# Attention scores of two batches on eight 32x64 tiles of the array, softmax and value products by pairs

## What is computed

```python
x = x + _L0(x, itok_B_1_198, weights0)          # a picked 32x32 matrix mixes the tokens of each batch
x = x + _L1(x, Wq, Wk, Wv, Wo, ..., k_blocks, v_blocks, block_tables, kv_lens)
x = x + _L2(x, itok_B_0_7, weights2)            # the same as L0 with another table
x = x + _L3(x, W, A, Bm, scalings, adapter)     # x W^T plus a low-rank adapter of rank 16

# _L1, attention over a paged cache: 8 heads in 4 groups of 2, 32 wide
q = _rope(_rms(q, q_norm_scale), pos); k = _rope(_rms(k, k_norm_scale), pos)
k_blocks = k_blocks.at[blk, :, off, :].set(k.transpose(0, 2, 1, 3))   # v_blocks too
scores = jnp.einsum('bghtd,bgsd->bghts', qg, k_all) * SCALE
allowed = (kpos <= pos) & (kpos > pos - 128)
p = jax.nn.softmax(jnp.where(allowed, scores, -jnp.inf), axis=-1)
o = jnp.einsum('bghts,bgsd->bghtd', p, v_all)
return jnp.einsum('bto,do->btd', o, Wo)
```

## Time and profile before

| | us |
|---|---|
| median of 3 runs | 550.79 |
| lowest and highest | 548.58, 552.23 |
| the profiled execution | 547.58 |
| its span (first to last instruction) | 545.8 |
| TensorE busy | 465.9 (85%) |
| VectorE busy | 404.1 (74%) |
| ScalarE busy | 341.7 (63%) |
| GpSimd busy | 209.5 (38%) |

### The profile page before, as it was taken

One profiled execution on the slowest core, in us unless ns is written; L12 is line 12 of the kernel. 1 busy time (PEld: TensorE's weight loads), 2 busy tenths in 40 slices (PEclk: granted clock), 3 DMA queues, 4 the chain that ended last, 5 costly groups with the idle time before them and its releaser, 6 DMA issues.

```text
span 545.8 us, 15661 instructions
## 1 busy us (share of the span) xinstructions
PE 465.9 (85%) x4726; PEld 388.8 (71%) x4726; DVE 404.1 (74%) x1357; ACT 341.7 (63%) x1075; POOL 209.5 (38%) x236
## 2 busy tenths in 40 slices
PE   0667999970026999999999999999999999999996
PEld 0556899960015788888878887887888888888884
DVE  7986478945116788888888888888888888878651
ACT  6166444555004687777877777777677786776662
POOL 7452688879604132422415223152341423212000
PEclk9999899995555899999999999999999999999999
DMA  7999566668266586768677696976968779755100
GB/s 228 293 335 377 174 220 196 193 187 184 82 154 127 139 177 168 170 154 168 165 147 173 144 174 156 152 175 136 170 165 153 170 144 178 173 122 114 22 22 19
DMA packets 87752, 90.10 MB, mean 165 GB/s; under 512 B 24199, under 2 KB 83623, under 8 KB 84940
## 3 DMA queue, kind: packets, MB, share of 16 engines
q1 hardware_dynamic: 72352, 52.58, 40.1%
q0 software_dynamic: 9312, 31.58, 24.4%
q10 hardware_dynamic: 6056, 5.54, 3.1%
HBM read 78.02 MB, written 35.65 MB: 208 GB/s over the span
## 4 chain that ended last, share of the span: by engine, by line
issue 46%; PE 12%; POOL 10%; DMA 3%; POOLq 1%; ACT 1%; DVE 0%; ACTq 0%; DVEq 0%
POOL old L862 4%; PE bank L1329 3%; DMA new<-written_blocks,g_idx 3%; POOL new L871 3%; POOL rms L828 3%; PE bank L1340 2%; PE bank L1355 2%; PE bank L1312 1%; POOL g_idx L855 1%; PE bank L1293 1%; PE bank L1307 1%; PE bank L1313 1%; PE bank L1330 1%; PE bank L1301 1%; PE bank L1288 0%
## 5 line engine op out<-in xcount | busy, mean ns | idle before, releaser
L828 POOL TENSOR_TENSOR rms<-rms,halfpow 128x8 f32<-128x8 f32 x48 | 85.6, 1783 | 232.6 <-DVE rms L576 232.6
L1131 ACT ACTIVATE p_room<-bank,nmax 128x176 f32<-128x176 f32 x256 | 101.4, 404 | 78.8 <-DVE nmax L704 67.1
L1329 PE MATMUL bank<-blocks_room,qbd 128*128 128x176 f32 x512 | 128.3, 355 | 3.4 <-issue 2.6
L1329 PEld LDWEIGHTS bank<-blocks_room,qbd 128*128 128x128 f32 x512 | 79.0, 195 | 22.7 <-issue 3.6
L704 DVE TENSOR_REDUCE nmax<-bank 128x2 f32<-128x352 f32 x128 | 66.7, 521 | 20.9 <-PE bank L1330 18.1
L1340 PE MATMUL bank<-ident,p_room 128*88 128x128 f32 x512 | 78.8, 277 | 3.2 <-DVE p_room L749 2.5
L1144 ACT ACTIVATE pT_room<-bank 88x512 f32<-88x512 f32 x128 | 75.2, 587 | 0.4 <-PE bank L1340 0.4
L749 DVE TENSOR_SCALAR p_room<-p_room,rrec 128x176 f32<-128x176 f32 x256 | 70.4, 317 | 5.6
L1340 PEld LDWEIGHTS bank<-ident,p_room 128*88 128x88 f32 x512 | 58.0, 124 | 14.7 <-DVE p_room L749 7.0
L1330 PE MATMUL bank<-pen,mask_sel 128*128 128x176 bf16 x256 | 62.2, 243 | 0.0
L1288 PE MATMUL bank<-ident,new 88*128 88x88 f32 x256 | 32.1, 252 | 33.3 <-DMA new<-written_blocks,g_idx 33.2
(11 more groups left out here) (199 smaller groups left out, 943.6 us busy)
## 6 DMA issues: line engine op xcount, KB each, us to landing
values_by_group<-new SPq DMA_DIRECT2D x16, 704.0 KB
blocks_room<-values_by_group SPq DMA_DIRECT2D x64, 88.0 KB
v_room<-values_by_group SPq DMA_DIRECT2D x64, 88.0 KB
xin<-in_x_dram SPq DMA_DIRECT2D x32, 128.0 KB
x_spill<-v_room SPq DMA_DIRECT2D x32, 128.0 KB
q_spill<-v_room SPq DMA_DIRECT2D x32, 128.0 KB
written_blocks<-new ACTq DMA_DIRECT2D x2, 2048.0 KB, 8.9
blocks_room<-q_spill SPq DMA_DIRECT2D x32, 128.0 KB
```

Source lines behind the costliest of these rows:

```text
L828: pool.tensor_tensor(out=rms[:, i, 2, :], in0=rms[:, i, 1, :], in1=halfpow[:, :], op=ALU.pow).then_inc(s_rstd, 1)
L1131: last = a.activation(pex[k % 2][:, h, :], ps_s[k % 2][:, h * KEYS:(h + 1) * KEYS], ACT.Exp, bias=nmax[:, k % 4, h:h + 1], accum_out=rsum[ ...
L1329: mm(dst, qbd[grp % 2][:, f, h, :], kT[grp % 2][:, f, :, :, :].rearrange("p c o w -> p (c o w)"), start=True, stop=False)
```

## The change

Slots now come in pairs: even slots compute the scores of two batches, odd slots turn their probabilities over.

- The scores of batches k and k+1 (L1336 and L1340 of the new code) use rows of the array by group and columns by batch: 8 tiles of 32x64 (32 values of a head dimension, 2 heads x 32 tokens), 176 columns each. A bank holds one group; the masks come first, one per bank, with weights of 128 and bf16. `qbd` with its zeros goes, `qT` is written with one copy per tile (L1163) in place of four.
- The four banks of a pair (`ps_u`) take its scores and then its transposed probabilities. So TensorE waits at the masks for both copies of the pair before (`s_ptc`), where it waited for an older exponential.
- Maxima of a pair are two instructions, one per half (two groups). The exponentials stay four per pair, and the transposes eight, of unnormalised probabilities `pex`.
- Normalisation moves behind the value products: VectorE spreads 1/sum over 32 columns (`rrep`), TensorE transposes it (L1377), ScalarE copies it per tile of four batches (`norm`, L1126), and VectorE multiplies the value products with it on their way out, where ScalarE copied them.
- The value products of a pair stand in the even slot behind the next pair's scores, 16 matrices of 88x32.
- The finishing steps come earlier, x2, x3, xa, x4 in slots 1, 2, 3, 0 of four; x3 is copied by VectorE. Keys are prepared in slots 1, 2, 3 and 5 and share one bank; x4, x3 and qT share another, x2 and xa the third. LAST is 133.
- ScalarE reorders values in slots 7 (two pieces) and 1 (two), both odd; VectorE as before.

The core of the diff:

```diff
+        pex = proom[:, 0:G * KEYS].rearrange("p (g k) -> p g k", g=G)
+        pT = troom[0:HK, :].rearrange("p (g c r) -> p g c r", g=G, c=2)
-        qbd = [sb(f"qbd{i}", [128, GB, HPG, 128]) for i in range(2)]
+        qT = [sb(f"qT{i}", [128, GB, HPG, C]) for i in range(2)]
-        ps_s, ps_p, ps_o, ps_m = ps[0:2], [ps[2], ps[4]], ps[5], [ps[6], ps[7], ps[3]]
+        ps_u = [ctx.enter_context(nc.psum_tensor(f"score_banks{i}", [128, 2, 512], f32)) for i in range(2)]
+        ps_o, ps_m = ps[5], [ps[6], ps[7], ps[4]]
-        PREP = {0: [("k0", None)], 1: [("k1", None)], 2: [("k2", None)], 3: [("qT", 0)], 4: [("k3", None)], 7: [("qT", 1)]}
+        PREP = {1: [("k0", None)], 2: [("k1", None)], 3: [("k2", None), ("qT", 0)], 5: [("k3", None)], 7: [("qT", 1)]}
-        FIN = {3: ("x2", 7), 0: ("x3", 8), 1: ("xa", 9), 2: ("x4", 10)}
+        FIN = {1: ("x2", 5), 2: ("x3", 6), 3: ("xa", 7), 0: ("x4", 8)}
+        BANK = {"x4": 0, "x3": 0, "qT": 0, "x2": 1, "xa": 1, "k0": 2, "k1": 2, "k2": 2, "k3": 2}
...
# VectorE
+                if k % 2 == 0 and 0 <= k < B:
+                    dve.wait_ge(s_qk, 8 * it + k // 2 + 1)
+                    for half in range(2):
+                        v.tensor_reduce(nmax[:, k // 2 % 2, 2 * half:2 * half + 2], ps_u[half][:, :, 0:KEYS], AX.X, ALU.max,
+                                        negate=True).then_inc(s_max, 1)
...
+                if k % 4 == 0 and 0 <= (k - 4) // 4 < NT:
+                    n = (k - 4) // 4
+                    dve.wait_ge(s_ntc, 4 * it + n + 1)
+                    dve.wait_ge(s_pv, 8 * it + 2 * n + 2)
+                    v.tensor_tensor(oT[n % 2][:, :, :, :].rearrange("p h f t -> p f h t"),
...
+                if k % 2 == 1 and 0 <= k < B:
+                    j = k // 2
+                    dve.wait_ge(s_exp, b + 1)
+                    v.reciprocal(rrec[:, j % 2, :], rsum[:, j % 2, :]).then_inc(s_rec, 1)
...
+                    v.tensor_copy(rrep[:, j % 2, :].rearrange("p (g d) -> p g d", g=G),
+                                  rrec[:, j % 2, :].unsqueeze(2).broadcast_to([128, G, HD])).then_inc(s_rrep, 1)
...
-                    for h in range(HPG):
-                        last = v.tensor_scalar(pn[k % 2][:, h, :], pex[k % 2][:, h, :], rrec[:, k % 4, h:h + 1], None, ALU.mult)
# ScalarE
+                if k % 4 == 0 and 0 <= (k - 4) // 4 < NT:
+                    n = (k - 4) // 4
+                    act.wait_ge(s_nt, 8 * it + 2 * n + 2)
...
+                    a.activation(norm[n % 2][:, :], ps_o[:, NORM_AT:2 * NORM_AT], ACT.Copy).then_inc(s_ntc, 1)
...
-                i, pieces = pieces_in_slot(k, {6: (0,), 7: (1,), 0: (2, 3)})
+                i, pieces = pieces_in_slot(k, {7: (0, 1), 1: (2, 3)})
# TensorE
-                        pe.wait_ge(s_exp, b - 1)
-                    for h in range(HPG):
-                        dst = ps_s[k % 2][:, h * KEYS:(h + 1) * KEYS]
-                        mm(dst, qbd[grp % 2][:, f, h, :], kT[grp % 2][:, f, :, :, :].rearrange("p c o w -> p (c o w)"), start=True, stop=False)
-                        last = mm(dst, mask_sel[:, k % 4, :], pen[n % 2][:, :], start=False, stop=True)
+                        pe.wait_ge(s_ptc, b)
+                    for g in range(G):
+                        mm(ps_u[g // 2][:, g % 2, 0:KEYS], mask_sel[:, k // 2 % 2, :], pen[n % 2][:, :], start=True, stop=False)
+                    for f2 in range(2):
+                        for g in range(G):
+                            rows = slice(HD * g, HD * g + HD)
+                            last = mm(ps_u[g // 2][HPG * C * f2:HPG * C * f2 + HPG * C, g % 2, 0:KEYS],
+                                      qT[grp % 2][rows, f + f2, :, :].rearrange("p h t -> p (h t)"),
+                                      kT[grp % 2][rows, f + f2, :, :, :].rearrange("p c o w -> p (c o w)"), start=False, stop=True)
...
+                    if kb % 4 == 2:
+                        pe.wait_ge(s_ntc, 4 * it + kb // 4 + 1)
```

172 lines of the change are left out of this document (83 added, 89 removed).

## The result

| | kernel before | kernel after |
|---|---|---|
| median of the runs | 551.46 us (4 runs, 548.58 to 552.23) | 544.06 us (4 runs, 542.20 to 544.34) |
| ratio | 1 | 0.988, 95% interval 0.984 to 0.993 |
| span of the profiled execution | 545.8 us | 540.5 us |
| fourteen groups of the middle | 319.9 us, 22.85 each | 314.3 us, 22.45 each |

The change gains 7.4 us. The prediction was 522 us, a gain of 29, in a range of 505 to 556. The direction was right, and 544 lies in the range, but three quarters of the expected gain are missing. The question of this part is where they went.

A forecast was written before the change was run, and what follows sets the result against it. TensorE's order of work was taken to set the pace. Groups falling from 22.94 to 21.0 us save 1.94 x 15 = 29 us: span 545.8 to 517, plus 5 for the median, 522 us; range 505 to 556.

The forecast's parts named there:

- Bound and form: Loop: TensorE's order of work sets the pace before; after, a pair's steps from scores to copy run in series.
- 4.68 forecast: Chain of one pair, masks and scores through the second half's copy: 4.68 us, against 5.74 before.
- Scores, 0.36: Score tiles of a pair on TensorE: two rounds of eight overlapping tiles plus issue, 0.36 us.
- an estimated 0.53: Scores of a pair by the skill's packing speedup, about 5.5x on 2.9 us: 0.7 us more per group than 0.36.
- the other sentence of the Trainium skill: Tiling speeds up TensorE but not PSUM's emptying; faster scores give at most 0.36 us per pair, 22 us.
- The single pairs: Four pairs of a group: 4 x 4.68 plus 0.53, 0.40, 0.53 and 0.63 not hidden, 20.8 us.
- The reorder's shadow, 0.63: ScalarE's moved reorder delays the norm copy, and TensorE's work queued behind it, by 0.63 us once per group.
- nothing by itself: VectorE loses 70.4 us of work and gets 45 us, stays under its present load, so costs nothing.
- The gather of the new blocks: Issued 10.7 us into a group, landing 14.7 (median) to 15.7 us later, needed in the next group's slot 1.
- the gather again: New blocks' gather keeps a group from going under 20.1 us (median landing) or 21.1 (longest); 21.0 taken.
- Rival (b): Gather lands later as shorter groups pack bytes closer: at 17 us, groups of 22.4, 543 us; chance 0.08.
- stay as they are: Outside the loop's groups, start and tail were taken as unchanged, adding nothing to the sum.

The follow-up runs named there:

- reorder_even: The changed kernel with ScalarE's value reorder pieces moved from slots 7 and 1 to slots 6, 7 and 0; 540.54 us, ratio 0.978.
- few_new: early_old with the loop's gathers of the new blocks fetching 8 rows of 88, so the output is wrong; 563.5 us.
- early_again: early_old unchanged, run again in another call on another chip; 563.32 us, ratio 1.017.
- few_rows: The changed kernel with the loop's gathers of the old blocks fetching 8 of 88 rows, so the output is wrong; 523.77 us.
- early_old: The changed kernel with the old blocks' gather issued ahead of the root on GpSimd, all 88 rows; 528.45 us, ratio 0.957.
- aligned: early_old with the old blocks' gather issued only behind VectorE's two maxima of slot 0; 525.65 us, ratio 0.957.
- before_early: The kernel before with the old blocks' gather issued ahead of the root on GpSimd; 549.8 us, ratio 0.9994.
- after_third: The changed kernel unchanged, timed again beside the kernel before in a later call; 543.50 us, ratio 0.986.
- seam: early_old with one trip less in the loop of 16 slots, those slots written out behind it; 556.4 us, repeated at 555.78 us.
- after_again: The changed kernel unchanged, run again in another call on another chip; 550.87 us, one run.
- call B: The second of five timing sessions, each on another chip; the kernel before had a median of 552.3 us in one session and 548.9 to 553.6 us across all.

## Why the prediction was right or wrong

**Bound and form: right.** TensorE set the pace before, and the two batches of a pair now go through scores, maximum, exponentials, transposes and copy in series. The releasers are those that were named, and the last pairs, where only the chain is left, take 4.81 to 4.85 us, against 4.68 forecast.

**Scores, 0.36: a little low.** 0.50 in the timeline and 0.5 to 0.6 when doubled. The row of the value products didn't show this. The other number in the prediction, an estimated 0.53 by the Trainium skill (TensorE: Matmul & The Clock Gate, "Part 3: Packing small matmuls"), was the better one; it is worth some 0.6 us per group. With the other sentence of the Trainium skill (TensorEngine Tiling (Array Packing), "PSUM Bottleneck") the trace agrees: at 77% TensorE waits for engines that empty PSUM.

**The single pairs: nearly right in sum, not in parts.** Forecast 5.84, 5.08, 5.21, 4.68, in all 20.8; measured 5.55, 4.90, 5.60, 5.16, in all 21.2. The reorder's shadow, 0.63, doesn't exist (reorder_even leaves the pair as it is). Instead the pairs of slots 4 and 5 and of 6 and 7 are longer than forecast, by 0.39 and 0.48: there TensorE waits for VectorE's spread reciprocals (L742, 0.3 us) and, before the masks, for the penalties (L695, up to 0.7 us). That VectorE's additions cost "nothing by itself" is thus the likeliest place of this 0.9 us; no run took it apart.

**The gather of the new blocks: near, and in two groups late.** It was issued 10.0 us after a group's start (forecast 10.7). Between 300 and 420 us it took 13.2 to 17.8 us to land, median 14.6, where the forecast's longest was 15.7, and TensorE waited for it in two groups, 2.3 us. That isn't a bound on every group. With 8 rows (few_new) the groups are no shorter than those of early_again, 23.7 to 26.0 against 23.6 to 24.3, both in calls of the second kind.

**What failed is the step "the gather again":** it bounded one of the two gathers. The other, of the old blocks, is issued behind the root on GpSimd, and its reader is VectorE in slot 6, in order and ahead of everything that the next pair needs: 11.3 us lie between them, and up to 14.4 were needed. Rival (b) named a late landing that must hold on average; in fact single late ones are enough, as each is passed on at once, and half a clock can follow it. With this gather early the long groups go but for pair 55's, 14 of the 24 missing us. It is shown by taking rows away (few_rows), by issuing earlier (early_old, aligned) and by the control on the kernel before (before_early). Of the 14, 8.9 stand in groups with this wait or the low clock behind it; that the late new blocks, values and queries of the other two groups come from the same late issue is inferred from their being gone in early_old; three profiles with the late issue have such waits (after, after_third, reorder_even).

Rival (b)'s 543 us and 22.4 per group are by luck what was measured (544 and 22.45): most groups were short and a few long, and it was mostly the other gather. The range held the result for the same reason. Pair 55's 2.5 us, where TensorE stops for nothing that the profile shows, had no term in the sum.

**Start and tail "stay as they are": wrong both ways.** The first layer waits for the transfer of bd. In four profiles of the kernel before TensorE starts it at 32.6 us; in fifteen of the changed kernel and its variants mostly at 36.3 to 37.6, but also at 29.3, 32.5, 33.6 and 35.1, the same program (seam) once at 37.35 and once at 33.56. It costs the 4.6 us of the start (the load of values that the first group waits for comes 4.5 us later, 172.13 instead of 167.63); why the transfer of bd is later is open. The four key transposes of the first group now share one bank and take 2.3 us longer, but this hides behind that load. The tail is chain alone: it and the last group gained 4.3 us, where the sum counted 1.9 for that group.

**On the two kinds of call** the prediction had nothing. In one of the second kind the changed kernel takes 551 us (one run) where before takes 553.

## What to carry to other kernels

When a change ties the engines into one chain, list every transfer with its issuer, what stands ahead of the issue in that queue, and its reader, and set the time between issue and reader against its longest landing, not only for the transfer that is nearest by name. A wait of 0.3 us in the trace of before is the warning. Time a change that rests on where GpSimd issues in more than one call, on more than one chip, and look in the trace where the issue falls: here one wait instruction moved it away from x3's copy, though not beside the exponentials, as meant.

## What was not expected of the hardware

- Around GpSimd's issue of an indirect gather (1.06 to 1.12 us, one of 1.57 in aligned), signals of TensorE to VectorE and ScalarE reach them in some calls up to 2.1 us late, in others in 0.18 and 0.11 us as ever. Most late ones come 0.2 to 0.65 us behind an issue's end, but the maxima of after_again start 0.3 us late while the issue still runs. It made the same program 528 us in one call and 563 in another, while the kernel before stayed at 549 to 554 (its groups in call B are 22.66 and 23.24 us, as in the first profile). What carries these signals and why calls differ isn't shown. The Trainium skill (SBUF — State Buffer, "Who interferes with whom") names only the port that VectorE and GpSimd share, and says that TensorE and ScalarE never wait for anyone. It speaks of access to SBUF; here ScalarE's copy out of PSUM began 1.07 us late, waiting for a signal, which the section doesn't cover. The Trainium skill also says (Perfetto Trace Analysis, "Per-engine timelines") that a matmul's reported end is computed, not observed, and that its signal goes out when PSUM has acknowledged the write: TensorE's rows would look punctual, as they do here, if that acknowledgement were late. No run tells whether it was.
- In a stream that is otherwise busy, a wait of TensorE of 0.9 to 2.7 us can be followed by 3.4 us at a granted clock of 0.5 (x4 2.07 instead of 1.10 us), and waits of 1.4 and 1.6 us were not.
- Eight fp32 tiles of 32x64 with 176 columns, two instructions each, take 0.50 us, 0.031 per instruction, where the two instructions of one 128-row score took 0.18.
- TensorE can stop for 4.7 us in the midst of equal matmuls, six slots behind a loop's end, in nine of fifteen profiles.
